# Two layers with attention and experts on one core: first batch's routing one pair earlier, expert weights split in pieces, first blocks opened inside attention

## The reference

```python
x = x + _L1_attn_ref(_layernorm(x, axis=-1), W_Q, W_K, W_V, W_O, b_Q, b_K, b_V, b_O)   # causal, 16 heads of 128
x = x + _L1_ffn_ref(_layernorm(x, axis=-1), router_weight, router_bias, gate_up_proj, ...)

def _L1_ffn_ref(hidden_states, ...):        # E, H, I = 8, 256, 256; TOP_K = 2
    logits = h @ router_weight.T + router_bias
    top_vals, top_idx = jax.lax.top_k(logits, TOP_K)
    top_w = jax.nn.softmax(top_vals, axis=-1)
    scores = zeros_like(logits).at[arange(T)[:, None], top_idx].set(top_w)
    gate_up = einsum('th,ehj->etj', h, gate_up_proj) + gate_up_proj_bias[:, None, :]
    gate, up = minimum(gate_up[..., ::2], 7.0), clip(gate_up[..., 1::2], -7.0, 7.0)
    act = (up + 1.0) * gate * sigmoid(gate * 1.702)
    expert_out = einsum('eti,eih->eth', act, down_proj) + down_proj_bias[:, None, :]
    return einsum('te,eth->th', scores, expert_out)
```

## Time and profile before

| | us |
|---|---|
| median of 3 runs | 1858.89 (1858.15 to 1863.1) |
| the profiled execution | 1863.42, its span 1861.70 |
| PE busy | 1606.7 (86%) |
| DVE busy | 1245.3 (67%) |
| ACT busy | 970.2 (52%) |
| POOL busy | 655.5 (35%) |
| attention ends on PE | about 1637 from the start of the span |
| first and last block of experts begin | 1646.31 and 1834.67 |

### The profile page before, as it was taken

One profiled execution on the slowest core, in us unless ns is written; L12 is line 12 of the kernel. 1 busy time (PEld: TensorE's weight loads), 2 busy tenths in 40 slices (PEclk: granted clock), 3 DMA queues, 4 the chain that ended last, 5 costly groups with the idle time before them and its releaser, 6 DMA issues.

```text
span 1861.7 us, 31205 instructions
## 1 busy us (share of the span) xinstructions
PE 1606.7 (86%) x9354; PEld 1337.9 (72%) x9354; DVE 1245.3 (67%) x2797; ACT 970.2 (52%) x2046; POOL 655.5 (35%) x727
## 2 busy tenths in 40 slices
PE   3578778788999989999999987999999999858795
PEld 2345444677788878888888886788888888746584
DVE  6677474678965666667666675766676666758485
ACT  3355354355533376666666754656676566523242
POOL 5133235533333332223222312332232322355652
PEclk9789788899999999999999998999999999979897
DMA  3000001100010330000000000010000000231243
GB/s 108 1 1 1 0 1 46 63 12 14 5 21 1 80 98 1 23 23 23 23 0 23 6 18 23 1 47 1 23 23 23 9 14 6 91 119 58 95 134 130
DMA packets 78383, 64.53 MB, mean 35 GB/s; under 512 B 16656, under 2 KB 72704, under 8 KB 78288
## 3 DMA queue, kind: packets, MB, share of 16 engines
q1 hardware_dynamic: 74544, 53.08, 10.1%
q0 software_dynamic: 3744, 10.26, 1.5%
HBM read 44.89 MB, written 18.43 MB: 34 GB/s over the span
## 4 chain that ended last, share of the span: by engine, by line
PE 63%; DVE 18%; issue 6%; ACT 5%; DVEq 3%; POOL 3%; DMA 1%; POOLq 0%; ACTq 0%; SPq 0%
PE psum L53 10%; PE psum L55 10%; PE psum L54 10%; PE psum L1691 6%; PE psum L1704 3%; PE psum L1707 3%; PE psum L1705 3%; PE psum L1681 3%; PE psum L1683 3%; PE psum L1682 3%; DVE table_leaves L589 2%; DVE mamba_conv_sum L1127 2%; POOL moe_slots_x L2172 2%; DVE mamba_mixed L1149 2%; PE psum L999 1%
## 5 line engine op out<-in xcount | busy, mean ns | idle before, releaser
L1887 POOL TENSOR_SCALAR attn_probs<-attn_probs,attn_inverse 128x128 f32<-128x128 f32 (+7 forms) x256 | 191.9, 750 | 533.8 <-DVE attn_inverse L1838 533.7
L1755 ACT ACTIVATE attn_pt_hi<-psum 128x512 fp32r<-128x512 f32 (+3 forms) x384 | 185.1, 483 | 168.3 <-PE psum L1691 168.2
L1760 ACT ACTIVATE attn_probs<-attn_probs,attn_neg_max 128x128 f32<-128x128 f32 (+7 forms) x256 | 198.4, 775 | 142.2 <-DVE attn_neg_max L1810 140.6
L1806 DVE TENSOR_TENSOR attn_pt_lo<-psum,attn_pt_hi 128x512 fp32r<-128x512 f32 (+3 forms) x384 | 211.6, 552 | 41.3 <-ACT attn_pt_hi L1755 38.6
L1691 PE MATMUL psum<-ident,attn_probs 128*128 128x128 f32 x1152 | 192.9, 277 | 17.8 <-DVE x_tok L1846 11.9
L1810 DVE CUSTOM_DVE_ANT_0 attn_probs<-psum,attn_mask 128x128 f32<-128x128 f32 (+7 forms) x256 | 192.5, 753 | 15.6 <-PE psum L1683 5.7
L1704 PE MATMUL psum<-attn_pt_hi,attn_v_hi 128*128 128x512 f32 (+3 forms) x384 | 161.4, 420 | 23.5 <-DVE attn_pt_lo L1806 13.7
L1691 PEld LDWEIGHTS psum<-ident,attn_probs 128*128 128x128 f32 x1152 | 142.7, 142 | 43.8 <-issue 12.9
L417 POOL TENSOR_TENSOR gated_h_lo<-gated_hidden,gated_h_hi 128x512 fp32r<-128x512 f32 x56 | 79.5, 1420 | 161.2 <-ACT gated_h_hi L402 161.2
L1707 PE MATMUL psum<-attn_pt_hi,attn_v_lo 128*128 128x512 f32 (+3 forms) x384 | 134.9, 351 | 0.0
L1681 PE MATMUL psum<-attn_k_hi,attn_q_hi 128*128 128x512 f32 (+3 forms) x384 | 132.1, 344 | 2.7 <-DVE attn_neg_max L1810 2.5
(11 more groups left out here) (380 smaller groups left out, 4773.8 us busy)
## 6 DMA issues: line engine op xcount, KB each, us to landing
moe_xrow<-moe_slots_x SPq DMA_DIRECT2D x46, 129.0 KB, 2.1
moe_slots_x<-attn_z_raw SPq DMA_DIRECT2D x4, 1032.0 KB, 12.9
attn_qkv_raw<-in_L_attn_W_Q_dram SPq DMA_DIRECT2D x32, 128.0 KB, 2.2
attn_qkv_raw<-in_L_attn_W_K_dram SPq DMA_DIRECT2D x32, 128.0 KB, 2.5
attn_qkv_raw<-in_L_attn_W_V_dram SPq DMA_DIRECT2D x32, 128.0 KB, 2.6
attn_wo_raw<-in_L_attn_W_O_dram SPq DMA_DIRECT2D x16, 256.0 KB, 3.1
moe_weights_raw<-_L_ffn_gate_up_proj_dram SPq DMA_DIRECT2D x8, 512.0 KB, 6.3
x_in<-_attn_hidden_states_dram SPq DMA_DIRECT2D x4, 512.0 KB, 5.6
```

The lines of the kernel that those rows point to most:

```text
L1760: act.activation(probs_view(e), probs_view(e), ACT.Exp, bias=stat(neg_max, e), scale=-1.0, accum_out=stat(sums, e)).then_inc(exp_done, 1)
L1806: dve.tensor_tensor(lo, work_view(e), hi.bitcast(F32), ALU.subtract).then_inc(work_done, 1)
L1887: pool.tensor_scalar(probs_view(e), probs_view(e), stat(inverse, e), 1.0, ALU.mult, ALU.mult).then_inc(probs_ready, 1)
```

## The change

- A fifth kind of section, `route`: in the second batch the loop covers pairs 1 to 5, and pair 6 is written out with the routing steps of the first batch that stood in `last`, closer together. SP's loads for that pair are written out with it.
- `last` carries twelve `moe_weights` pieces instead, one behind each chunk from 11 to 22: experts 0 to 3 in three pieces of 512 columns each, the high part by ACT, the low part by POOL. The weights are laid out so that gate/up and down lie side by side; the factor 0.5 on the down weights goes into the row weights (2.0 in `weigh`) and into the down bias (one more ACT step in `bias_scalar`).
- Experts 4 to 7 are split whole, 1536 columns, ACT and then POOL, in iterations 2 to 5. DVE makes no low part of weights any more.
- `moe_open`: behind chunk 20 of `last` the row blocks 0 and 1 are turned, split and given their own rows; ahead of the pair's last output products PE does the gate/up products of block 0.
- `own` rows come from ACT instead of POOL.
- SP loads experts 0 and 1 after turn 4 of `last`, four row blocks and experts 2 and 3 after turn 11, experts 4 and 5 when attention is done, experts 6 and 7 two row loads later. The first batch's output is stored before the second batch's results are read back.
- `LATE` is packed: norm to weights in iterations 0 to 11, then one scatter step of two indirect DMAs in each of iterations 11 to 18.

```diff
-                  last={1: [("moe_first", 0)], 4: [("moe_second", 0)], 6: [("moe_bias", 0)], 7: [("moe_ranks", 0)],
-                        9: [("moe_blocks", 0)], 10: [("moe_place", 0)], 11: [("moe_weigh", 0)], 12: [("moe_scatter", 0)],
-                        13: [("moe_scatter", 1), ("moe_experts", 0)], 14: [("moe_scatter", 2)], 15: [("moe_scatter", 3)],
-                        17: [("moe_scatter", 4)], 18: [("moe_scatter", 5)], 19: [("moe_scatter", 6)],
-                        20: [("moe_scatter", 7), ("moe_weights", 0)], 22: [("moe_weights", 1)]})
+                  route={1: [("moe_first", 0)], 3: [("moe_second", 0)], 5: [("moe_bias", 0)], 6: [("moe_ranks", 0)],
+                         7: [("moe_blocks", 0)], 8: [("moe_place", 0)], 9: [("moe_weigh", 0)], 10: [("moe_scatter", 0)],
+                         11: [("moe_scatter", 1), ("moe_experts", 0)], 12: [("moe_scatter", 2)], 13: [("moe_scatter", 3)],
+                         16: [("moe_scatter", 4)], 18: [("moe_scatter", 5)], 20: [("moe_scatter", 6)],
+                         22: [("moe_scatter", 7)]},
+                  last={**{11 + n: [("moe_weights", n)] for n in range(12)}})
+    MOE_AT["last"][20].append(("moe_open", 0))
+    BODIES = (PAIRS - 2, PAIRS - 3)
+    kinds = ("first", "start", "body", "route", "last")
...
+            if last and b:
+                events.append(dict(what="moe_open", m=1))
             if last:
                 for t in range(HALF, QT // 2):
                     output(t, 4)
...
+            if b:
+                load_qkv(PAIRS - 1)
+                load_wo(PAIRS - 2)
...
-        dve.tensor_scalar(best[0][:, :], ratio[:, :], 1.0, None, ALU.add)
+        dve.tensor_scalar(best[0][:, :], ratio[:, :], 1.0, 2.0, ALU.add, ALU.mult)
...
-    def high(self, act, e):
+    def high(self, act, e, part=0, parts=1):
+        n = self.half // parts
         act.wait_ge(self.loaded[e // 2], 64)
...
+        act.activation(self.part(e, part * n, n), self.raw_part(e, self.half + part * n, n), ACT.Copy).then_inc(self.split_hi, 1)
+
+    def low(self, pool, e, part=0, parts=1):
+        n = self.half // parts
+        lo, raw, hi = (f(e, at + part * n, n) for f, at in ((self.part, self.half), (self.raw_part, self.half), (self.part, 0)))
+        done = self.PIECES * e + part + 1 if e < self.EARLY else self.pieces_to(e)
+        pool.wait_ge(self.split_hi, done)
+        pool.tensor_tensor(lo, raw, hi.bitcast(F32), ALU.subtract).then_inc(self.split_lo, 1)
...
-    LATE = {0: [("stats", 0)], 1: [("apply", 0)], 2: [("stats", 1), ("turn", 0)], 3: [("apply", 1), ("turn", 1)], 4: [("turn", 2)],
-            5: [("turn", 3)], 6: [("rows", 0)], 7: [("rows", 1)], 8: [("logits", 0)], 9: [("first", 0)], 10: [("second", 0)],
-            11: [("ranks", 0)], 12: [("blocks", 0)], 13: [("place", 0)], 14: [("weigh", 0), ("experts", 0)],
-            15: [("scatter", 0)], 16: [("scatter", 1)], 17: [("scatter", 2)], 18: [("scatter", 3)]}
+    LATE = {0: [("stats", 0)], 1: [("apply", 0), ("stats", 1)], 2: [("turn", 0), ("apply", 1)], 3: [("turn", 1)], 4: [("turn", 2)],
+            5: [("turn", 3), ("rows", 0)], 6: [("rows", 1)], 7: [("logits", 0), ("first", 0)], 8: [("second", 0)],
+            9: [("ranks", 0), ("blocks", 0)], 10: [("place", 0)], 11: [("weigh", 0), ("scatter", 0)],
+            12: [("experts", 0), ("scatter", 1)], **{11 + m: [("scatter", m)] for m in range(2, 8)}}
-    FIRST_AHEAD = 2
+    FIRST, FIRST_AHEAD = weights.EARLY, 2
...
+        sp.wait_ge(*attention["tail"][1])
         for n in range(XS):
             load(n)
+        weights.load(sp, a, 1)
         sp.wait_ge(*attention["done"])
-        for n in range(2, EXPERTS // 2):
-            weights.load(sp, a, n)
+        weights.load(sp, a, 2)
         for n in range(XS, N):
             load(n)
+            if n == XS + 1:
+                weights.load(sp, a, 3)
...
+        sp.wait_ge(added, PARTS)
+        sp.dma_start(out_dram[:, 0:TB, :], s.x[:, 0:TB, :]).then_inc(out_stored, 16)
         for p in range(PARTS):
             load_back(1, p)
...
+    def own_rows(act, n):
...
+        act.activation(own[:, n % OR, :], s.ones[:, :], ACT.Copy, scale=r.sel[:, b, j:j + 1]).then_inc(own_ready, 1)
...
+    def open_tensor(pe, part):
+        if part == 0:
+            pe.wait_ge(*attention["scores_read"])
+            for n in range(2):
+                load_expert(pe, n)
+                turn_rows(pe, n)
+        else:
+            gate_up(pe, 0)
+
+    def open_scalar(act, part):
+        if part == 0:
+            for n in range(2):
+                own_rows(act, n)
+                high_rows(act, n)
+
+    def open_vector(dve, part):
+        if part == 0:
+            for n in range(2):
+                low_rows(dve, n)
```

208 lines of the change are left out of this document (96 added, 112 removed).

## The result

The changed kernel takes 1828.63 us (median of 4 runs, 1826.51 to 1832.51) against 1858.52 for the kernel before in the same comparison (1857.58 to 1863.1, 4 runs): ratio 0.9833, 95% interval 0.9811 to 0.9856. Forecast was 1824, range 1810 to 1840. The sum came out close, but not by its own terms: routing in the written-out pair costs 12.4 us where 4.5 were forecast, more than the 10 that the prediction named as its sign of being wrong, and three later stretches give back more than forecast.

What follows compares the result with a forecast made beforehand. PE was taken to bound attention and the experts from block 23 on, with PE waiting in between. Terms 4.5 - 8.7 - 22.3 - 6.5 - 1.5 = -34.5 us took the median from 1858.89 to 1824, range 1810 to 1840.

Steps and rivals of the forecast that it cites:

- (a): Routing in the written-out pair before the last: a loss of 4.5 us, ends 0 and +10.
- (b): Last pair without routing, with weight splits and block 0's products added: -8.7 us, ends -4 and -11.
- (c): Attention's end to block 8: 40 us instead of 62.3, so -22.3 us, ends 28 and 53.
- the three quarters of my sum: Up to block 8, DVE's two-operand operations wait for three quarters of a POOL low part: 2.7 of 3.55 us.
- (d): Blocks 8 to 23: 63.3 us instead of 69.79 by the earlier, packed second-batch routing, so -6.5 us.
- (e): Blocks 23 to 45: PE-bound, nothing changes, 0 us.
- (f): The tail: the first batch's 1 MB output goes out earlier, -1.5 us, within 0 to 3 us.
- The first: Rival: POOL's low parts don't hold up DVE before block 8, that stretch takes 28 us, total 1812; chance 0.17.
- The second: Rival: blocks 1 to 7 keep nearly the old 6.6 us each, routing costs its pair 10, total 1837; chance 0.17.
- The third: Rival: opened blocks and split pieces queue on ACT in the last pair, attention ends unchanged, total about 1845; chance 0.05.
- the fourth: Rival: DVE's steps starve PE in the written-out pair, its clock stays at 1.2 GHz, total about 1881; chance 0.05.

Runs made afterwards that it cites:

- e1_bias_low_later: Changed kernel with DVE's part of the bias split five chunks later, behind chunk 10 instead of 5; median 1830.18 us, ratio 0.9831, routed pair 70.04 us.
- e12_clear: Changed kernel, routing over two written-out pairs, none behind chunks 7-11 or 19-23, earlier scatters, ACT's late step first, experts 4-7 in 512-column pieces; 1821.35 us, ratio 0.9821.
- e2_spread: Changed kernel with whole routing steps spread over the routed pair, last scatter in the last pair; median 1827.44 us, ratio 0.9817, routed pair 69.03 us.
- e9_two_pairs: Changed kernel with routing's 34 DVE operations over written-out pairs 5 and 6, none behind chunks 8 to 11 or 20 to 23; median 1830.16 us, ratio 0.9843.
- e4_routing_earlier_only: Kernel before with only pair 6 written out and the first batch's routing steps moved into it; median 1855.58 us, ratio 0.9973.
- e8_open_after: Changed kernel with blocks 0 and 1 opened behind attention's last output products instead of inside the last pair; median 1835.95 us, ratio 0.9860.
- e6_low_memset: Changed kernel with GpSimd filling the low parts of experts 4 to 7 with zeros instead of subtracting; median 1827.52 us, ratio 0.9820.

## Why the prediction was right, and where its steps were not

**(a), the step that failed.** The pair lost 12.4 us, beyond the 10 from which the prediction called itself wrong; that the total came out so near is luck, as later terms erred the other way by 6.3 us. The step took the price of routing from the pair half in which it stood, 5.04 us, and took DVE's 19.5 idle microseconds as room in the new pair. But the last pair's halves have 3.4 us of PE slack (21.51 of 24.90), the routed pair 1.7 (57.34 of 59.03). Routing's 37 operations kept DVE busy for 9.67 us in the last pair of before and 10.77 in the routed pair. With 1.4 us for the wait on ACT's bias work (e1_bias_low_later), 0.7 of PE's own for the ranks and at most 1.7 for the fallen clock (0.17 of ten microseconds), which the sum left out, and less the 1.7 of slack, that makes 12.9, near the 12.4. It is an estimate that prices each microsecond of DVE at one of PE's; no run shows it. The upper end, 10, was too low as well. Nor is that price a law: e12_clear paid 6.7 us for 11.5 us of such work in two pairs, at most 1.7 of it for the clock, and twelve operations behind chunks 0 to 6 of its pair 6 cost no more than 0.5 up to chunk 11. Spreading the steps (e2_spread, 10.0 us) and cutting them over two pairs (e9_two_pairs, 10.1), both at a clock of 1.00, saved little beyond what the clock may have cost. Idle time of DVE is room only where PE's lead covers it. What stays open is how much of the last 5 us belongs to the place and how much to the amount.

**(b)** -8.37 for -8.7: the clock went from 0.80 to 1.00 as reckoned, PE did not wait for weights, and block 0's products stand in the gap. But the clock did not come back by moving the routing alone: e4_routing_earlier_only and e8_open_after, which leave that gap open, ended the pair at 0.93, with 6.4 and 7.0 us gained instead of 8.4. So the opening, which the sum had as a cost of 1.2, seems to have brought 1.4 to 2, in one trace each.

**(c)** 38.16 to block 8, where 40 was forecast, from two wrong terms that nearly cancel. DVE's own work was 27.0 us (27.6 forecast). The lock took 5.5 of DVE's time (12 forecast): DVE meets a subtraction once in each of four iterations, not twice, and stands from where it comes until GpSimd is done, not for three quarters of its length. (Here one engine is held up by another with no semaphore between them, other than the first section says.) The rows of before had it already: the 2.43 us began 0.47 behind POOL's 2.35 and ended 0.55 behind them. In the three L2600 above, DVE ends 0.28 to 0.29 us behind POOL (1661.74 and 1661.46, 1666.57 and 1666.28, 1671.27 and 1670.98). The other 5.6 us are DVE's waits, for which 0.5 stood in the sum; two of 1.3 us are for act_hi behind ACT's weights. The Trainium skill, page "SBUF — State Buffer", section "SBUF: two separate sides", says that whichever starts first holds the shared pair for its whole instruction and the other fully blocks. These rows agree; the three quarters of my sum don't.

**(d)** -9.63 for -6.5. The first part was right: weights 19.1 us behind block 8 (19.5 forecast). The rest took 41.1 instead of 43.8: POOL's part 34.5 instead of 36.0, as both taggings were shorter and stores between scatters cost 1.26 us each like them, not 1.34; and what follows the last scatter, up to block 23, 6.6 instead of 7.75. DVE's and POOL's rows at the two ends of POOL's part:
```profile
1693.75 0.17 DVE L2157 TENSOR_TENSOR moe_weight<-moe_ratio,moe_weight 128x8 f32<-128x8 f32 x1
```
```profile
1727.00 0.96 POOL L2187 DMA_INDIRECT moe_slots_x<-moe_rows,moe_slot_i  x1 [0.30 <-issue]
```

**(e), (f)** 0.16 for 0, and -2.83 for -1.5, within its bounds of 0 to -3; no run took the early output store back by itself, so this term is not shown.

**The rivals.** The first (DVE not held up) falls by the stretched rows and by e6_low_memset; its 12 us were worth at most 3.3. The second came nearer with the price of routing (10, measured 12.4) and had the pace of the blocks wrong. The third didn't come. Of the fourth there is little: the clock of the routed pair is 0.98, at most 1.7 us.

## What to carry to other kernels

Work that moves to an engine with idle time is priced by the slack of the engine that waits for it, at the place where it lands, not by its price where it stood; reading a lag against an undisturbed turn of the same loop shows that place. Cutting whole steps of 1.5 to 2.3 us into single operations brought little (10.1 us lost instead of 12.4); the same operations kept off the narrow stretches as well lost 6.7. A removed wait is worth nothing where the next lock or queue takes its time. Terms of a sum should be held against the trace one by one even when the total is right: here +7.9 and -6.3 nearly hid each other, by luck.

## What the runs showed of the hardware

A GpSimd operation with one SBUF tensor (the scaling L1900) holds up DVE operations as a subtraction of two does: 2.46 us for L1855 beside two in a row instead of 0.69, and an operation of 64 columns took 0.81 us beside one instead of 0.22, where the next took 1.19 beside a subtraction.

The clock can fall for a few microseconds behind a short wait, at the same place in one run and not in another. Windows of block 22 to 23, first e2_spread at 0.62 (a mix of 2.4 and 1.2 GHz), then the changed kernel at 1.00:
```profile
1731.65:1736.09 4.44, 4.44 (x20) 3.81 (x20) 1.71 (x5) 0.96 (x3) 0.96 (x1) 0.62 0.48 151
```
```profile
1731.94:1734.83 2.89, 2.89 (x20) 2.58 (x20) 1.25 (x4) 0.91 (x3) 0.96 (x1) 1.00 0.78 247
```
PE's wait ahead was 1.99 us in the first and 2.19 in the second, so the runs don't show what decides; the price is 1.55 us. A difference below 2 us between two traces at unequal clock is therefore not shown by them alone, other than in the stretch to block 8, which kept its length at clocks of 0.82 and 0.91 (38.15 and 38.17 us).
